# Reordering the front, the end of a scan chain and the norm behind it in a two-layer recurrent, attention and gated kernel

## The reference

```python
xn = layernorm(x)
x  = x + L0_attn(xn) + L0_ffn(xn)   # recurrent memory + one expert (relu MLP)
xn = layernorm(x)
x  = x + L1_attn(xn) + L1_ffn(xn)   # rotary causal attention + gated 512-wide MLP
# L0_attn, token by token, M is 64 x 128:
#   k = elu(Wk r) + 1;  v = Wv r;  r = rmsnorm(xn) * norm_weight
#   M = layernorm_of_whole_matrix(M + eta * |v - k M| * outer(k, v))
#   output: xn + Wout (q M_final),  q = elu(Wq r) + 1
```

## Time and profile before

| what | value |
|---|---|
| time before, median of 3 runs | 256.51 us (256.14 to 256.53) |
| the profiled execution | 256.91 us |
| its span, first to last instruction | 255.1 us |
| PE busy | 245.0 us (96%) |
| DVE busy | 204.5 us (80%) |
| ACT busy | 185.8 us (73%) |
| POOL busy | 115.0 us (45%) |

### The profile page before, as it was taken

One profiled execution on the slowest core, in us unless ns is written; L12 is line 12 of the kernel. 1 busy time (PEld: TensorE's weight loads), 2 busy tenths in 40 slices (PEclk: granted clock), 3 DMA queues, 4 the chain that ended last, 5 costly groups with the idle time before them and its releaser, 6 DMA issues.

```text
span 255.1 us, 5149 instructions
## 1 busy us (share of the span) xinstructions
PE 245.0 (96%) x1669; PEld 160.1 (63%) x1673; DVE 204.5 (80%) x681; ACT 185.8 (73%) x460; POOL 115.0 (45%) x150
## 2 busy tenths in 40 slices
PE   7899998999998999999999999999999999999993
PEld 2359554776764477786778767886875444444492
DVE  7888899999958998998899887787613996666674
ACT  2697789976637887887667899989814997777730
POOL 9789700000004589887755994997790000000000
PEclk9999999999999999999999999999999999999999
DMA  6620000000008403000000000000000000000004
GB/s 189 187 81 3 1 0 3 1 0 3 3 3 321 177 15 149 3 1 0 4 0 3 0 0 3 1 1 0 4 3 0 0 0 3 0 1 0 1 29 141
DMA packets 8479, 8.50 MB, mean 33 GB/s; under 512 B 1793, under 2 KB 7554, under 8 KB 7938
## 3 DMA queue, kind: packets, MB, share of 16 engines
q1 hardware_dynamic: 7074, 7.52, 8.8%
q10 hardware_dynamic: 1376, 0.62, 0.9%
HBM read 7.09 MB, written 1.05 MB: 32 GB/s over the span
## 4 chain that ended last, share of the span: by engine, by line
PE 63%; DVE 20%; POOL 6%; ACT 3%; issue 3%; DMA 2%; DVEq 0%; SPq 0%; POOLq 0%; ACTq 0%
PE PS L957 11%; PE PS L956 11%; PE PS L929 8%; PE PS L906 7%; PE PS L919 4%; POOL arena L1497 3%; POOL arena L1498 3%; PE PS L718 3%; DMA x<-L_attn_x 2%; PE PS L672 2%; PE PS L726 2%; DVE mxb L2022 2%; DVE arena L2008 2%; PE PS L575 2%; PE PS L570 2%
## 5 line engine op out<-in xcount | busy, mean ns | idle before, releaser
L956 PE MATMUL PS<-arena 128*128 128x512 f16 x128 | 48.5, 379 | 0.0
L957 PE MATMUL PS<-arena 128*128 128x512 f16 x128 | 48.5, 379 | 0.0
L2080 DVE TENSOR_TENSOR arena<-arena 128x512 f32<-128x512 f32 x32 | 22.2, 693 | 13.0 <-ACT arena L1416 13.0
L906 PE MATMUL PS<-arena 128*128 128x512 f32 (+3 forms) x80 | 31.9, 530 | 0.3 <-ACT arena L1385 0.3
L1415 ACT ACTIVATE arena<-PS,arena 128x512 f32<-128x512 f32 x32 | 22.9, 715 | 9.1 <-PE PS L957 9.1
L1497 POOL TENSOR_TENSOR arena<-arena 128x256 f32<-128x256 f32 x32 | 21.5, 672 | 15.7 <-DVE arena L2014 13.1
L1385 ACT ACTIVATE arena<-PS,lnt 128x512 f32<-128x512 f32 (+3 forms) x40 | 24.8, 628 | 3.2 <-DVE lnt L2029 3.2
L1498 POOL TENSOR_TENSOR arena<-arena,small 128x256 f16<-128x256 f32 (+1 forms) x36 | 23.8, 660 | 2.8
L1505 POOL CAST arena<-arena 128x512 f16<-128x512 f32 x2 | 1.3, 637 | 49.1 <-ACT x L1278 49.1
L1416 ACT ACTIVATE arena<-PS,arena 128x512 f16<-128x512 f32 x32 | 22.8, 712 | 0.0
L2022 DVE TENSOR_REDUCE mxb<-PS 128x1 f32<-128x512 f32 (+3 forms) x40 | 22.1, 601 | 0.0
(11 more groups left out here) (292 smaller groups left out, 614.5 us busy)
## 6 DMA issues: line engine op xcount, KB each, us to landing
arena<-h_T SPq DMA_DIRECT2D x2, 1024.0 KB, 5.9
arena<-cos SPq DMA_DIRECT2D x1, 1024.0 KB, 4.8
arena<-sin SPq DMA_DIRECT2D x1, 1024.0 KB, 6.8
arena<-w_T SPq DMA_DIRECT2D x3, 256.0 KB, 3.1
x<-L_attn_x SPq DMA_DIRECT2D x2, 256.0 KB, 5.5
out<-arena SPq DMA_DIRECT2D x2, 256.0 KB, 2.2
x<-L_attn_x SPq DMA_DIRECT2D x2, 128.0 KB, 2.6
x<-L_attn_x ACTq DMA_DIRECT2D x2, 128.0 KB, 3.2
```

Of the source, the lines that this page charges most:

```text
L906: i = mm(PS[:, k, 0:cnt * P], qT1[:, t * P:(t + 1) * P], kT1[:, c * P:(c + cnt) * P], start=True, stop=not last)
L956: mm(bank(b), wH[:, k, m * P:(m + 1) * P], sH[:, k, cols], start=(k == 0), stop=False)
L957: i = mm(bank(b), wL[:, k, m * P:(m + 1) * P], sL[:, k, cols], start=False, stop=(k == HT4 - 1))
L2080: v.tensor_tensor(RP[m], FP[m], high, ALU.subtract).then_inc(rest_ready, 1)
```

## The change

Front: the first `rms_normed` on DVE comes before all of the third chunk's statistics. `wvT` is loaded by SP ahead of the chunks 2 and 3 of `x`, `normw` by ACT in its place. Chain: `last_rows` one step later; `WVO` copied at step 19; one reciprocal and `c0` inside the chain at steps 13 and 18, so that the query pieces come one step later; PE's filler at step 25 is gone. Chain end: the guard runs before the last query pieces, and pieces 12 to 15 are replaced by one minimum in place and four more matmuls. PE reads the flag between the two halves of the memory's output. Norm: half of the next chunk's statistics before `shifts`, the first rotation before the last `shifts`; another order of copies on ACT; PE transposes the next chunk between `turn` and `skip`. POOL's key sum waits for DVE's query sum. The rotary tables lie elsewhere in `arena` and are loaded during the chain; two small mask copies and five small DVE instructions move forward; `high` copies move back.

```diff
-        cosT, sinT = arena[:, a_tab:a_tab + T], arena[:, a_tab + T:a_tab + 2 * T]
+        cosT = Gf[:, S:S + T]
+        sinT = arena[:, at[0]:at[0] + T]
-        LAST_AT = 15
+        LAST_AT = 16
@@ sync
+            sp.dma_start(wvT[:], a["WvT"]).then_inc(early_in, 16)
             for c in range(2, 4):
                 sp.dma_start(x[:, 4 * c:4 * c + 4, :], ...)
-            sp.dma_start(normw[:], ...).then_inc(early_in, 16)
...
-            sp.wait_ge(x1_ready, 2)
-            for i, n in enumerate(("cos", "sin")):
-                sp.dma_start((cosT, sinT)[i], a[n]).then_inc(tab_in, 16)
+            sp.wait_ge(lanes_act, 10)
+            sp.dma_start(cosT, a["cos"]).then_inc(tab_in, 16)
+            sp.wait_ge(tables_ready, 1)
+            sp.wait_ge(terms_act, 2)
+            sp.dma_start(sinT, a["sin"]).then_inc(tab_in, 16)
@@ tensor
             def memory_output(two, first, end):
-                    pe.wait_ge(q_ready, 2 * (4 * two + k + 1))
+                    pe.wait_ge(q_ready, (11, 13, 13, 13)[k] if two else 2 * (k + 1))
+                    if two and k >= 2:
+                        for c in (2, 3):
+                            mm(PS[:, c, k * P:(k + 1) * P], QE[...], MW[...], start=False, stop=False)
...
-                elif EO_AT[-1] + 4 < j < L - 2:
-                    keep_warm(4, 4)
+                if j == EO_AT[-1]:
+                    pe.wait_ge(c0_ready, 1)
+                    mm(PS[0:W, 5, HALF:HALF + REST], ..., c0[0:W - 1, 0:REST], ...).then_inc(shift_done, 1)
...
             keep_warm(1, 4)
-            pe.wait_ge(rh_ready, 1)
+            pe.wait_ge(rh_ready, 2)
             mm(PS[:, 6, HALF:HALF + 1], ..., rh[:, 1:2], ...)
+            pe.wait_ge(c0_ready, 2)
+            mm(PS[0:W, 5, HALF + REST:HALF + REST + 1], ..., c0[0:W - 1, REST:REST + 1], ...).then_inc(shift_done, 1)
+            keep_warm(1, 4)
             pe.wait_ge(uw_ready, 1)
             mm(PS[:, 7, 0:D], UW, VW, start=True, stop=True).then_inc(mw_done, 1)
+            keep_warm(1, 4)
+            pe.wait_ge(guard_ready, 2)
+            mm(PS[0:1, 5, 1:2], agree, ...).then_inc(count_done, 1)
+            keep_warm(1, 4)
             pe.wait_ge(mw_act, 1)
             memory_output(0, 0, 2)
-            pe.wait_ge(agree_ready, 1)
-            mm(PS[0:1, 5, 1:2], agree, ...).then_inc(count_done, 1)
...
             memory_output(0, 2, 4)
+            keep_warm(1, 4)
+            general_path(pe, general)
             memory_output(1, 0, 4)
-            keep_warm(4, 4)
-            general_path(pe, general)
-            keep_warm(7, 4)
+            keep_warm(3, 4)
...
             def normed(c):
-                pe.wait_ge(xn2_act, 2 * c + 2)
-                pe.wait_ge(xn2_dve, 2 * c + 2)
-                for n in range(4 * c, 4 * c + 4):
+                for k in range(4):
+                    n = 4 * c + (2, 0, 3, 1)[k]
+                    pe.wait_ge(xn2_act if k % 2 else xn2_dve, 2 * c + k // 2 + 1)
                     i = tr(...)
             def projected(c):
-                if c == 0:
-                    normed(1)
+                if c < 3:
+                    normed(c + 1)
@@ scalar
-            act.dma_start(wvT[:], a["WvT"]).then_inc(early_in, 16)
+            act.dma_start(normw[:], ...).then_inc(early_in, 16)
...
+                if j == LAST_AT + 3:
+                    act.wait_ge(wvo_done, 1)
+                    f(WVO, PS[:, 7, 0:D], ACT.Copy).then_inc(wvo_act, 1)
...
             f(MW, PS[:, 7, 0:D], ACT.Copy, scale=rhb).then_inc(mw_act, 1)
+            f(ident_b, ident, ACT.Copy).then_inc(mask_act, 1)
+            f(causal_b, con[:, C_CAUSAL:C_CAUSAL + P], ACT.Copy).then_inc(mask_act, 1)
...
             first_block(2)
+            transposed(0)
             deviations(1)
-            transposed(0)
+            normed(1)
             first_block(3)
-            normed(1)
             deviations(2)
+            transposed(1)
             normed(2)
-            transposed(1)
             deviations(3)
+            skipped(0)
+            transposed(2)
             normed(3)
-            transposed(2)
+            skipped(1)
+            transposed(3)
...
-                if t < 2:
-                    high(t + 2)
+                if t < 3:
+                    high(t + 1)
@@ gpsimd
-                pool.wait_ge(rope_dve, 2 * c + 2)
+                pool.wait_ge(turned_dve, c + 1)
@@ vector
             variances_in(0)
-            chunk_statistics(2, 0, 2)
             rms_normed(0)
-            chunk_statistics(2, 2, 4)
+            chunk_statistics(2)
             chunk_statistics(3)
...
+                    dve.wait_ge(h_ready, REST)
+                    v.reciprocal(rh[:, 0:1], HS[:, REST:REST + 1])
...
-                    if j >= LATENT:
-                        query_sums(j - LATENT)
+                    if j == LATENT:
+                        v.scalar_tensor_tensor(out=c0[:, 0:REST], ...).then_inc(c0_ready, 1)
+                    if j > LATENT:
+                        query_sums(j - LATENT - 1)
...
-            query_sums(9, 10)
+            query_sums(8)
+            v.tensor_scalar(QE[:, BANK + ZC:2 * BANK], QE[:, BANK + ZC:2 * BANK], 1.0, None, ALU.min).then_inc(q_ready, 1)
             dve.wait_ge(h_ready, L)
-            v.reciprocal(rh, HS[:, REST:L + 1:HALF]).then_inc(rh_ready, 1)
...
-            query_sums(11, 12, 13, 14, 15)
...
...
+            query_sums(9, 10, 11)
             dve.wait_ge(count_done, 1)
...
-            for c in range(4):
-                shifts(c)
-                normed(c)
-                if c < 3:
-                    statistics(c + 1)
-                    variances(c + 1)
+            for c in range(4):
+                if c < 3:
+                    statistics(c + 1, 0)
+                else:
+                    rotated(0)
+                shifts(c)
+                normed(c)
+                if c < 3:
+                    statistics(c + 1, 1)
+                    variances(c + 1)
+            rotary_sum(0)
+            rotated(1)
+            rotary_sum(1)
+            for c in range(2, 4):
+                rotated(c)
+                rotary_sum(c)
```

More of the change, by code:

```diff
@@ L241, in program @@
         assert max(b_at[0], at[0]) <= 44992, (b_at, at)
-        TURN = [hBf[:, T * c:T * c + 2 * BANK].rearrange("p (k t) -> p k t", k=2) for c in range(2)]
+        TURN = [hAf[:, 2 * T + 2 * BANK * c:2 * T + 2 * BANK * (c + 1)].rearrange("p (k t) -> p k t", k=2) for c in range(2)]
         xd = hBf[:, T + 2 * BANK:T + 3 * BANK]
@@ L754, in memory_output @@
                 for k in range(first, end):
-                    pe.wait_ge(q_ready, 2 * (4 * two + k + 1))
+                    pe.wait_ge(q_ready, (11, 13, 13, 13)[k] if two else 2 * (k + 1))
+                    part = slice((4 * two + k) * P, (4 * two + k + 1) * P)
+                    if two and k >= 2:
+                        for c in (2, 3):
+                            h0 = F * (c % 2)
+                            mm(PS[:, c, k * P:(k + 1) * P], QE[h0:h0 + F, part], MW[h0:h0 + F, :], start=False, stop=False)
@@ L756, in memory_output @@
                     for c in (2 * two, 2 * two + 1):
                         h0 = F * (c % 2)
-                        i = mm(PS[:, c, k * P:(k + 1) * P], QT[h0:h0 + F, (4 * two + k) * P:(4 * two + k + 1) * P], MW[h0:h0 + F, :], start=False, stop=(k == 3))
+                        i = mm(PS[:, c, k * P:(k + 1) * P], QT[h0:h0 + F, part], MW[h0:h0 + F, :], start=False, stop=(k == 3))
                         if k == 3:
-                            i.then_inc(ao_done, 1)
-            for j in range(FAR + 1, L):
+                            i.then_inc(ao_late if two else ao_done, 1)
@@ L781, in _ @@
+            keep_warm(1, 4)
             pe.wait_ge(mw_act, 1)
             memory_output(0, 0, 2)
-            pe.wait_ge(agree_ready, 1)
-            mm(PS[0:1, 5, 1:2], agree, con[:, C_ONES:C_ONES + 1], start=True, stop=True).then_inc(count_done, 1)
             def general():
@@ L862, in _ @@
                 projected(c)
-                for n in ((2,), (3,), (), ())[c]:
-                    normed(n)
             values(0)
@@ L1138, in queries @@
                 if linear:
-                    f(QT[:, cols], bank(Q_BANK[b]), ACT.Copy).then_inc(qphi_act, 1)
+                    f(QT[:, cols], bank(Q_BANK[b]), ACT.Relu, bias=minus_one).then_inc(qphi_act, 1)
                 else:
@@ L1251, in _ @@
                     behind(k)
-            act.wait_ge(wvo_done, 1)
-            f(WVO, PS[:, 7, 0:D], ACT.Copy).then_inc(wvo_act, 1)
-            act.wait_ge(rhb_done, 1)
+            act.wait_ge(ends_done, 3)
             n = o.did(f(rhb, PS[:, 6, HALF:HALF + 1], ACT.Copy))
@@ L1299, in high, with skipped @@
                 f(xH[:, c * BANK:(c + 1) * BANK], xT[:, c * BANK:(c + 1) * BANK], ACT.Copy).then_inc(xh_act, 1)
+            def skipped(c):
+                b = 4 * ((c + 1) % 2)
+                cols = slice(c * BANK, (c + 1) * BANK)
+                act.wait_ge(skip_done, c + 1)
```

(16 more changed lines are left out.)

96 lines of the change are left out of this document (44 added, 52 removed).

## The result

The changed kernel takes 254.96 us, median of 6 runs (254.87 to 255.64), the kernel before 256.46 us in 6 runs on the same chip (256.14 to 256.93). The ratio is 0.9942, with a 95% interval of 0.993 to 0.9954. That is 1.5 us faster, where 3.2 us were forecast. The sign was right; the size was not, and the time lies just above the end of the range (254.9). The step that failed is the largest of the sum, the norm: 1.5 us were forecast for DVE's idle times there, and 0.8 came, because PE was already full in the same stretch.

A forecast was written before the change was run, and what follows sets the result against it. It took waits through DVE and ACT, a late flag, then DVE's norm as the bound. Gains 0.45 + 0.2 + 1.15 + 1.5 = 3.3 us gave 253.6 from the profile, 253.2 from the median; forecast 253.3, range 252.7 to 254.9.

The forecast's parts named there:

- Point 1: Front: first rms_normed ahead of the third chunk's statistics fills DVE's transfer wait; gain 0.45 us, bounds 0.1 to 0.5.
- Point 2: Before the chain: five small DVE instructions moved into DVE's wait for ACT cost nothing there; 0 us.
- Point 3: Chain: last_rows a step later removes ACT's wait for PE, the moved reciprocal loses about 0.1; gain 0.2 us.
- Points 3 and 4: Chain and flag: earlier UW and guard set the flag 1.37 us earlier, 0.2 the chain's; bounds 1.0 to 1.45.
- The tie of flag and banks: Chain end: PE's first two banks and the work behind the branch both come at 73.0 us, limiting further flag gains.
- Point 5: Norm and rotation: DVE's idle times filled and small instructions removed; gain 1.5 us, bounds 1.1 to 1.7.
- Point 6: Norm: POOL's key sum behind DVE's query sum moves its end by 0.1 us; counted as 0.
- Point 7: Chain: rotary tables loaded during it do not slow it; 0 us.
- (a): Partial loss at a second limit: PE's branch, POOL's add or chunk 2; together 254.7 us; chance 0.24 shared with (d).
- (b): Norm gain lost later, in the gates, where changed interleaving could hold a tile; 254.7 us, chance 0.08.
- (c): Slower: PE's granted clock falls in the norm stage, at worst 262.5 us; chance 0.04.
- (d): Chain end: guard misses its turn in PE's queue, flag only 0.43 us earlier; 254.1 us, chance 0.24 shared with (a).

The follow-up runs named there:

- the best kernel: Changed kernel with the key half of ACT's first unrotated copies behind transposed(2), no filler before the memory's output, six satisfied DVE waits: 254.59 us, ratio 0.9917.
- three of the experiments: Changed kernel with POOL's casts after one bank (255.14 us); casts after four tiles plus three other edits (255.12); ACT's whole unrotated pair behind transposed(2) (255.81).
- a fourth: Changed kernel with split ACT copies, no filler before the memory's output, six satisfied DVE waits, and POOL's casts held for six DVE tiles: 254.87 us, ratio 0.9919.

## Why the prediction was right in sign and wrong in size

**Point 1, front, +0.45; measured +0.1 against an early execution, about +0.36 by the runs. Right in kind, doubtful in its base.** The idle time of 0.72 us was that of one execution; run again it was 0.26 us, and ACT's root leaves 0.29 us in any case. For the median of 256.5 us, against which the forecast was made, one delay was probably counted twice: the profiled execution was 0.4 us above it, the prediction took these 0.4 us off at the end as belonging to nothing, and it booked 0.45 us of gain for removing what they most likely were. In the later runs of the kernel before, with medians of 256.7 to 256.9 us, the late landing would be the usual one, and most of the 0.45 us would be there. This fits the 1.5 us of the first comparison and the 1.9 of the second, but without traces of these runs it is not shown.

**Point 2, small instructions moved:** nothing is seen of them, as forecast.

**Point 3, chain, +0.2; measured -0.1.** `last_rows` a step later brought 0.17 us of the 0.31 counted, the reciprocal cost 0.08 of the 0.1 counted. Together these are +0.1, within the bounds. What was not in the sum is the stop of 0.23 us at step 9, which comes with another number of instructions ahead of it.

**Points 3 and 4, flag.** The flag comes 0.96 us earlier against the last scan; the forecast's own steps make that 1.17 (from 69.47 to 71.85, where before it was from 69.67 to 73.22). From the last scan to `UW` it said 0.88 and 0.91 came (69.22 to 70.13). From `UW` to the subtraction it said 0.35, and 0.48 came, 0.21 of it a wait for PE's shift of the second column of `c0`, which comes only after `c0` itself. From there to the flag's end 1.13 was said and 1.18 came. Another 0.1 is PE's filler behind the count. The tie of flag and banks was forecast at 73.0, and the banks end at 73.06.

**Point 5, norm, +1.5; measured +0.8. This is the step that failed**, and the largest part of what is missing in the pair of traces (0.7 of 1.8 us; the front is 0.35, chain and chain end together 0.6, the rest 0.1). The forecast took DVE's chain for the stage's. On DVE's side its bounds of 1.1 to 1.7 held: the last rotary sum ends 18.60 us behind the first statistics before and 17.40 after, a gain of 1.2. Of the 1.9 us removed, 0.23 went to ACT's root in `shifts(1)`, which was forecast, 0.16 to a wait for ACT's copy of the bank, 0.38 to the tile held beside POOL. But then DVE waits 0.46 us for PE's first scores, and the stage gains 0.8.

PE was the second limit already before. The row stood in the text with 9.26 of 10 us, for the clock only; it does not show the limit by itself, as it holds 3.0 us of filler. In the stretch from the first projection to the first scores no filler starts. First the kernel before, run again, then the changed kernel:

```profile
78.73:92.04 13.31, 13.25 (x45) 6.61 (x45) 12.18 (x43) 11.42 (x24) 9.58 (x8) 1.00 0.49 204
77.20:90.47 13.27, 13.12 (x46) 6.47 (x45) 12.55 (x38) 10.68 (x23) 7.92 (x7) 1.00 0.23 80
```

Before, PE was busy for 13.25 of the 13.31 us, and DVE and PE came to the first score together: DVE's last sum ended at 92.51 and PE's score product at 92.48. The trace that the prediction was made from says the same (13.24 of 13.31 us). So from the first projection on, a gain on DVE could shorten the stage only as far as PE's own stretch shrank, and that went from 13.31 to 13.27 us, in the best kernel to 13.07. The norm's gain is, to within 0.1 us, what the first projection won: 4.82 us behind the first statistics before, 4.11 after, 0.71 us.

**Point 6, POOL's key sum, 0; in the new order 0.7 us.** The reading of the earlier trace rows was right: 1.77 is not the instruction's own length, behind DVE's sum it is 1.27 us (forecast 1.17). Wrong was to cost the edit against the old order of DVE's work. There DVE's sum followed its product at once and was first; in the new order POOL would be first, once. Without this edit, the others would have brought a little over half as much (ratio 0.9957, not 0.9922).

**Point 7, tables:** no step of the chain besides 9 and 14 is longer, and step 9's stop is not theirs. The 0 stands.

**Rivals.** (a), a second limit, is what happened, though at PE's full time in the norm and not at PE's branch, POOL's add or chunk 2. (b), the gain lost later: nearly nothing in the changed kernel (0.1 us), but 0.4 to 0.5 us in three of the experiments and 0.2 in a fourth. (c), the clock: no slice fell. (d) did not happen: the flag was 0.96 us earlier against the last scan.

**A better version?** The three edits together (half pair behind, no filler, six waits) gave 254.59 us, 0.9917 (0.9903 to 0.993), beside 254.88 and 0.9922 (0.9909 to 0.9936) of the changed kernel. The spans are 252.9 and 253.1 us. It is no worse, and not to be told apart.

## What to carry to other kernels

Before a sum is made from one engine's idle times in a stage, read the other engines' busy time in the same stretch, without fillers: a stretch in which PE is busy for 13.25 of 13.31 us gives at most what is idle there, plus what its first work comes earlier. Before a wait in the front is booked as a gain, compare the profiled execution with the median of enough runs; if it is a late one, the wait is in the difference already, and one trace can mislead either way. And when work on DVE is moved, ask anew at every instruction of POOL beside it which of the two now starts first.

## What was not expected of the hardware

- A stop of 0.23 us in DVE's stream (0.17 at the other place), at a fixed place among its instructions, in both traces of the changed kernel and in all those that share its stream; with six more waits ahead it is gone at step 9 and one is at step 24, in all four traces.
- A difference of less than 0.2 us in who starts first, DVE or POOL, decides 0.5 to 1 us: DVE's f32 to f16 copy of 128x256 takes 0.29 us first and 0.77 us second; its 64x512 sum 0.69 us first and 1.66 us second. A pair of 128x128 `tensor_scalar` beside POOL's cast and scaling took 0.38 us more, though the scaling lasts 1.50; that is less than the whole instruction that the Trainium skill names (SBUF — State Buffer, Who interferes with whom). In the kernel before, pairs that started within the scaling were not held at all, and why no run shows.
- From the flag's start to the first instruction behind the branch 1.31 us pass on DVE in the kernel before (72.60 to 73.91) and without the filler (71.72 to 73.03).
- The landing of the same transfer of `x` made DVE wait 0.72 us in one execution and 0.26 us in another of the same kernel, and the whole span moves with it.
